# Output projection of an attention layer: four blocks at the end of a strip, or one after every second head pair of the next strip

## The reference

```python
x = x + attn(layernorm(x))     # 16 heads of 64, causal, width 1024, 2048 tokens
x = x + ffn(layernorm(x))      # activations quantised to 8 bits, weights to {-1, 0, 1}

# attn
q, k, v = x @ Q_w + Q_b, x @ K_w + K_b, x @ V_w + V_b      # per head
logits = q k^T / sqrt(64);  causal mask;  scores = softmax(logits)
attn = scores @ v
return einsum('bqhd,hdm->bqm', attn, O_w) + O_b            # the output projection
```

## Time and profile before

| | us |
|---|---|
| median of 2 runs | 4601.35 (4590.81 to 4611.88) |
| profiled execution | 4576.53 |
| its span, slowest core (core 5) | 4575.0 |
| the other cores | 4530.7 to 4571.6 |
| mean granted TensorE clock, by core | 0.748 to 0.753 of full speed |
| TensorE matmuls busy | 2803.8 (61% of the span) |
| VectorE busy | 1714.8 (37%) |
| ScalarE busy | 1032.6 (23%) |

### The profile page before, as it was taken

The page is one execution under the profiler, slowest core; times in us unless marked ns, Lnnn a source line. Parts: engine busy times, 40 slices in busy tenths (PEclk is TensorE's granted clock), DMA queues, the critical chain, the costliest instruction groups (busy, mean ns, idle before and its releaser), DMA issues. The chain is left out here.

```text
span 4575.0 us, 49341 instructions; the slowest of 8 cores (4530.7 to 4575.0 us)
## 1 busy us (share of the span) xinstructions
PE 2803.8 (61%) x17576; PEld 1453.1 (32%) x17576; DVE 1714.8 (37%) x3961; ACT 1032.6 (23%) x1127; POOL 45.5 (1%) x68
## 2 busy tenths in 40 slices
PE   0078557778712126767776377567778447778675
PEld 0023123334311114444442133133334234445342
DVE  1121243332233455645555122232111446564643
ACT  0001024447421131001010011024647231111010
POOL 0000000000000000000000000000000000000000
PEclk9988656665655559889898788665665678989889
DMA  7610022111164203445454410000000023545444
GB/s 125 175 33 19 19 92 83 66 61 42 48 173 141 107 19 78 121 120 147 120 148 136 154 32 14 19 28 6 15 19 1 10 42 83 148 123 150 128 129 156
DMA packets 472110, 380.91 MB, mean 83 GB/s; under 512 B 340674, under 2 KB 373570, under 8 KB 466756
## 3 DMA queue, kind: packets, MB, share of 16 engines
q1 hardware_dynamic: 460612, 335.81, 25.8%
q0 software_dynamic: 11264, 41.95, 2.9%
HBM read 335.77 MB, written 41.94 MB: 83 GB/s over the span
## 5 line engine op out<-in xcount | busy, mean ns | idle before, releaser
L80 ACT ACTIVATE b_pt<-b_lp,b_cb 128x1024 bf16<-128x1024 f32 (+3 forms) x640 | 622.1, 986 | 556.7 <-PE b_lp L80 355.2
L80 PE MATMUL c_op<-c_w2b,c_hq 128*128 128x512 bf16 x2048 | 516.9, 398 | 250.4 <-DMA c_w2b<-w2t_s 187.5
L80 PE MATMUL c_hp<-c_xq,c_w1b 128*128 128x257 bf16 x4096 | 521.4, 282 | 66.9 <-ACT c_H L80 58.3
L80 PE MATMUL b_av<-V,b_pt 128*128 128x65 bf16 x5120 | 376.9, 237 | 208.1 <-ACT b_pt L80 146.9
L80 PEld LDWEIGHTS c_hp<-c_xq,c_w1b 128*128 128x128 bf16 x4096 | 408.9, 101 | 203.1 <-issue 103.7
L80 ACT ACTIVATE c_H<-c_hp,c_cb 128x512 bf16<-128x512 f32 x256 | 175.9, 687 | 1249.4 <-DVE c_H L80 598.2
L80 PEld LDWEIGHTS b_av<-V,b_pt 128*128 128x128 bf16 x5120 | 296.1, 124 | 421.4 <-issue 421.3
L80 PE MATMUL b_lp<-Q,K 64*128 64x512 bf16 x1280 | 369.2, 589 | 11.0 <-DVE x L80 9.3
L80 PEld LDWEIGHTS c_op<-c_w2b,c_hq 128*128 128x128 bf16 x2048 | 197.6, 101 | 547.3 <-issue 354.0
L80 DVE TENSOR_TENSOR c_H<-c_hp,c_g1b 128x514 bf16<-128x514 f32 x256 | 176.8, 691 | 466.6 <-PE c_hp L80 465.9
L80 DVE MEMSET b_pt<- 128x256 bf16 (+2 forms) x192 | 93.1, 485 | 621.7 <-PE b_lp L80 551.5
(11 more groups left out here) (124 smaller groups left out, 2443.2 us busy)
## 6 DMA issues: line engine op xcount, KB each, us to landing
c_w2b<-w2t_s SPq DMA_DIRECT2D x256, 512.0 KB, 5.3
c_w1b<-w1t_s SPq DMA_DIRECT2D x128, 512.0 KB, 4.3
pw_stg<-w SPq DMA_DIRECT2D x32, 1024.0 KB, 4.9
wq_st<-w SPq DMA_DIRECT2D x16, 2048.0 KB, 9.1
a_xt<-x SPq DMA_DIRECT2D x32, 512.0 KB, 3.5
b_xr<-x SPq DMA_DIRECT2D x32, 512.0 KB, 3.6
out<-c_obf POOLq DMA_DIRECT2D x32, 512.0 KB, 3.3
wq_s<-p_wbf POOLq DMA_DIRECT2D x16, 512.0 KB, 8.0
```

What stands on the lines that cost most here:

```text
L80: h = getattr(eng, en["name"])(*en["args"], **en["kwargs"])
```

## The change

The attention buffer `atok` keeps its size in bytes but becomes two halves of bf16, one for each parity of the strip, so that a strip can be normalised into one half while the other is projected. The four blocks at the end of a strip go into a function, `emit_oproj(pp, v, rg)`. In strips 1 to 3, after pairs 0, 2, 4 and 6, one block of the strip before is emitted; after the last strip its own four follow. A block uses one region of `AVps2` (`rg`, always 0) for both the transposes and the output, no longer `Lps`; a list `reg_free` holds for each region the VectorE count from which it is free. The transposes are bf16 matmuls against the bf16 identity. The condition on `ve_x2` in `emit_logits` (line 612) stays in the text; it now refers to the last block of the strip before, or to none in strip 1. The wait of a new region's first AV matmuls, on `reg_free`, takes the place of those on `ve_pn2` and `ve_aT2`.

```diff
@@ -529,7 +529,7 @@
         qsq = es_b.enter_context(nc.sbuf_tensor(f"b_sq{s}", [128, 512], BF16))
         smf = es_b.enter_context(nc.sbuf_tensor(f"b_sm{s}", [128, 16], F32))
         ptil = es_b.enter_context(nc.sbuf_tensor(f"b_pt{s}", [128, 2048], BF16))
-        atok = es_b.enter_context(nc.sbuf_tensor(f"b_at{s}", [128, 4 * 1024], F32))
+        atok = es_b.enter_context(nc.sbuf_tensor(f"b_at{s}", [128, 2 * 4096], BF16))
         attT = es_b.enter_context(nc.sbuf_tensor(f"b_tt{s}", [128, 1024], BF16))
         zrec = es_b.enter_context(nc.sbuf_tensor(f"b_zr{s}", [128, 8], F32))
         xre = es_b.enter_context(nc.sbuf_tensor(f"b_xr{s}", [128, 2 * D], F32))
@@ -592,8 +592,7 @@
                 nc.psum_tensor(f"b_av{s}", [128, 2048], F32))
             sc_exp = [0, 0]
             ve_pn = 0
-            ve_pn2 = [0, 0]
-            ve_aT2 = 0
+            reg_free = [0, 0]
             ve_x2 = 0
             tn_tT = 0
             dl_x = [0] * NT
@@ -601,6 +600,51 @@
                 dl_x[u] = dlb[u % 2].inc(r.sync.dma_start(
                     out=xre[:, (u % 2) * D:(u % 2 + 1) * D],
                     in_=t_x[s, u * 128:(u + 1) * 128, :]), 16)
+            def emit_oproj(pp, v, rg):
+                nonlocal ve_x2, tn_tT
+                u = 4 * pp + v
+                ah2 = (pp % 2) * 4096
+                rb = rg * 1024
+                r.wait(r.tensor, ve, ve_pn)
+                r.wait(r.tensor, ve, reg_free[rg])
+                for c in range(8):
+                    tn.inc(r.tensor.matmul(
+                        AVps2[:, rb + c * 128:rb + (c + 1) * 128],
+                        atok[:, ah2 + v * 1024 + c * 128:
+                             ah2 + v * 1024 + (c + 1) * 128],
+                        ident_bf[:, :], start=True, stop=True,
+                        skip_group_check=True))
+                tn_tT = tn.v
+                r.wait(r.vector, tn, tn_tT)
+                ve_aT = ve.inc(r.vector.tensor_copy(
+                    attT[:, :], AVps2[:, rb:rb + 1024]))
+                r.wait(r.tensor, ve, ve_aT)
+                for half in range(2):
+                    hs = half * 512
+                    for c in range(8):
+                        tn.inc(r.tensor.matmul(
+                            AVps2[:, rb + hs:rb + hs + 512],
+                            attT[:, c * 128:(c + 1) * 128],
+                            OWb[:, c * 1024 + hs:c * 1024 + hs + 512],
+                            start=(c == 0), stop=False))
+                    tn.inc(r.tensor.matmul(
+                        AVps2[:, rb + hs:rb + hs + 512], ones1b[0:1, :],
+                        ob_row[0:1, hs:hs + 512], start=False, stop=True))
+                tn_o = tn.v
+                r.wait(r.vector, tn, tn_o)
+                r.wait(r.vector, dlb[u % 2], dl_x[u])
+                ve_x2 = ve.inc(r.vector.tensor_add(
+                    x2[:, u * D:(u + 1) * D],
+                    xre[:, (u % 2) * D:(u % 2 + 1) * D],
+                    AVps2[:, rb:rb + 1024]))
+                reg_free[rg] = ve_x2
+                nu = u + 2
+                if nu < NT:
+                    r.wait(r.sync, ve, ve_x2)
+                    dl_x[nu] = dlb[nu % 2].inc(r.sync.dma_start(
+                        out=xre[:, (nu % 2) * D:(nu % 2 + 1) * D],
+                        in_=t_x[s, nu * 128:(nu + 1) * 128, :]), 16)
+
             if s == 0:
                 stats_load(0)
                 stats_load(1)
@@ -668,9 +712,7 @@
                                 AF.Exp, scale=0.125, bias=Cbias[:, hp:hp + 1]))
                         r.wait(r.tensor, sc, sc_exp[lb])
                         if kc == 0:
-                            r.wait(r.tensor, ve, ve_pn2[hp % 2])
-                            if hp < 2 and p > 0:
-                                r.wait(r.tensor, ve, ve_aT2)
+                            r.wait(r.tensor, ve, reg_free[hp % 2])
                         ab = (hp % 2) * 1024
                         for hh in range(2):
                             for qs in range(4):
@@ -693,57 +735,22 @@
                         bass.AP(AVps2[:, :].tensor, ab + 64,
                                 [[2048, 128], [512, 2], [65, 4], [1, 1]])))
                     ve.inc(r.vector.drain())
+                    ah = (p % 2) * 4096
                     for hh in range(2):
                         for qs in range(4):
                             ve_pn = ve.inc(r.vector.tensor_single_scalar(
-                                atok[:, qs * 1024 + (2 * hp + hh) * 64:
-                                     qs * 1024 + (2 * hp + hh + 1) * 64],
+                                atok[:, ah + qs * 1024 + (2 * hp + hh) * 64:
+                                     ah + qs * 1024 + (2 * hp + hh + 1) * 64],
                                 AVps2[:, ab + hh * 512 + qs * 65:
                                       ab + hh * 512 + qs * 65 + 64],
                                 zrec[:, hh * 4 + qs:hh * 4 + qs + 1], ALU.mult))
-                    ve_pn2[hp % 2] = ve_pn
+                    reg_free[hp % 2] = ve_pn
                     if s == 0:
                         stats_step(p * 8 + hp)
-                for v in range(4):
-                    u = 4 * p + v
-                    r.wait(r.tensor, ve, ve_pn)
-                    r.wait(r.tensor, sc, sc.v)
-                    if v == 0:
-                        r.wait(r.tensor, ve, ve_x2)
-                    for c in range(8):
-                        tn.inc(r.tensor.transpose(
-                            AVps2[:, c * 128:(c + 1) * 128],
-                            atok[:, v * 1024 + c * 128:v * 1024 + (c + 1) * 128],
-                            ident_f32[:, :]))
-                    tn_tT = tn.v
-                    r.wait(r.vector, tn, tn_tT)
-                    ve_aT = ve.inc(r.vector.tensor_copy(attT[:, :],
-                                                        AVps2[:, 0:1024]))
-                    ve_aT2 = ve_aT
-                    r.wait(r.tensor, ve, ve_aT)
-                    for half in range(2):
-                        hs = half * 512
-                        for c in range(8):
-                            tn.inc(r.tensor.matmul(
-                                Lps[:, hs:hs + 512],
-                                attT[:, c * 128:(c + 1) * 128],
-                                OWb[:, c * 1024 + hs:c * 1024 + hs + 512],
-                                start=(c == 0), stop=False))
-                        tn.inc(r.tensor.matmul(
-                            Lps[:, hs:hs + 512], ones1b[0:1, :],
-                            ob_row[0:1, hs:hs + 512], start=False, stop=True))
-                    tn_o = tn.v
-                    r.wait(r.vector, tn, tn_o)
-                    r.wait(r.vector, dlb[u % 2], dl_x[u])
-                    ve_x2 = ve.inc(r.vector.tensor_add(
-                        x2[:, u * D:(u + 1) * D],
-                        xre[:, (u % 2) * D:(u % 2 + 1) * D], Lps[:, 0:1024]))
-                    nu = u + 2
-                    if nu < NT:
-                        r.wait(r.sync, ve, ve_x2)
-                        dl_x[nu] = dlb[nu % 2].inc(r.sync.dma_start(
-                            out=xre[:, (nu % 2) * D:(nu % 2 + 1) * D],
-                            in_=t_x[s, nu * 128:(nu + 1) * 128, :]), 16)
+                    if p >= 1 and hp % 2 == 0:
+                        emit_oproj(p - 1, hp // 2, 0)
+            for v in range(4):
+                emit_oproj(NP - 1, v, 0)
             if s == 0:
                 for n in range(NP * 8, 32):
                     stats_step(n)
```

## The result

The changed kernel is slower by 0.66%: the ratio to the kernel before is 1.0066, 95% interval 1.0045 to 1.0086, with medians of 4620.2 and 4588.3 us over 33 and 32 runs. (In some executions, whatever the kernel, the cores of one die run at a lower granted clock and take longer; the ratios leave such executions out, the medians don't, and of the last experiment's profile cores 0 to 3 alone are read, for this reason.) The forecast was 1.6%, or 74 us; measured are some 30. The direction was right, and the forecast more than twice the measured size.

What follows compares the result with a forecast made beforehand. ScalarE and TensorE wait in turn with nothing queued ahead for ScalarE, so blocks between pairs cost their whole time. Terms -210.3 + 285.4 - 5.4 + 4.4 = +74 us, scaled to 4676 us; range 4630 to 4712 us.

Steps and rivals of the forecast that it cites:

- What bounds the stage: Attention stage: nothing is queued ahead for ScalarE at a pair's end, so work put there adds its whole time.
- The 24 blocks: After pairs 0, 2, 4, 6 of strips 1 to 3: each copies a burst's first block, together +285.4 us.
- bf16 in the normalisation at no cost: Normalisation writing bf16, eight instructions of 1.63 us in all: taken as 0, bounds 0 and -19 us.
- After a block: Pair behind a block: no wait for the add, clock still high, 0.3 us gained at 18 more places, -5.4 us.
- The last burst: End of each sequence: one region makes transposes wait for the add, 0.9 us more a later block; +4.4 us in all.
- rival C: Strips 1 to 3: blocks keep the clock high through attention, -40 us, 4561 us, 0.9% faster; chance 10%.
- Rival B: Single blocks: clock stays low through every block, 13 to 13.9 us each, +117 us, 4719 us, 2.6% slower; chance 15%.
- Rival D: Blocks between pairs: hidden behind busy ScalarE, nearly all 210 us gone, 4390 us, 4.6% faster; chance 3%.

Runs made afterwards that it cites:

- the last experiment: `spread_halves` plus useless matmuls in pairs of strips 1 to 3, four ahead of the first AV matmuls and two on the diagonal: ratio 0.943, median 4318.0 us.
- spread_halves: Changed kernel with each block dealt out inside two pairs, between key blocks, and the last burst alternating regions: ratio 0.9548, median 4367.0 us, stage time 1035.8 us.
- experiment 2: Kernel before, with block output in the AV tile's second region, so the next logits don't wait for the add: ratio 0.996, stage time 1223.0 us.
- experiment 3: Experiment 2's kernel with six or twelve useless matmuls behind each burst between strips: stage time 1224.2 or 1235.2 us, against 1223.0 without.
- experiment 1: Changed kernel, with the logits behind each block waiting for the block's add again: ratio 1.025 to the kernel before, stage time 1333.4 us.
- experiment 4: Changed kernel with eight useless matmuls behind each of the 24 blocks: stage time 1325.3 us, +57.4 us.
- experiment 5: Experiment 2's kernel with useless matmuls in pairs of strips 1 to 3, at start and diagonal, then start only: stage times 1108.8 and 1110.9 us, against 1223.0.

## Why the prediction was right and wrong, point by point

- **What bounds the stage: right.** Nothing is queued for ScalarE at a pair's end, so a block there is paid whole. `spread_halves` shows it from the other side: with the same work behind queued logits the stages take 201 us less than with the bursts, part of it by the higher clock.
- **The 24 blocks: right.** +285.4 forecast, +279.3 measured; single ones 10.4 to 12.8 us over the cores. The first block of a burst was a good copy of them, to the reduction that hides the faster transposes in sequence 0. The eight bf16 matmuls took 1.01 us, as the bf16 transposes of the earlier trace rows at the low clock, and being plain matmuls did not bring the rise nearer: it came 4.5 us after a block's first output matmul in the mean, 4.4 us before the change. (The prediction says that no row has a transpose in transpose mode; those of the earlier trace rows are `transpose` calls of the program, and whether they use that mode the trace doesn't show.)
- **bf16 in the normalisation at no cost: right.** 276 ns an instruction in the mean, before and after.
- **"After a block": wrong, and this is the miss.** I priced the high clock behind a block by the six pairs behind bursts, 0.3 us each. It is about 2 us, 47 us in all instead of 5. The two other errors, 6 us too much for the blocks and 5 too little for the last bursts, cancel by luck. The step took a burst to be a stronger form of a block ("after 28 us of dense matmuls it lasted under ten microseconds of attention"). Experiments 2 and 3 show that it isn't: what ends the high clock is mostly the idle time at a pair's start (experiments 1, 4 and 5), and whether that does it depends on where the start lies to the rise. All bursts ended at about the same distance from their rise (22 to 24 us), so six equal rows were nearer to one observation than to six.
- **The skill's rule.** The Trainium skill ("TensorE: Matmul & The Clock Gate", "Loop structure matters more than you think") says that a long DMA wait between matmuls costs the clock, a copy on VectorE between dense stretches none. By it I had rival C, at 10%. The trace of after agrees in part: clock 0.69 over 700 to 1210 us, where the kernel before has 0.61 there. C was half true: its mechanism acted in the typical case, up to the pair's end and not beyond; that it did not turn the direction of the result is partly luck, for it hung on where the pairs' starts lay. Its price for a pair at full clock, 8%, was also low: 15.1 against 17.5 us (experiment 5) is 14%.
- **The last burst:** +4.4 forecast, +9.4 measured. The wait for the region was sized rightly (0.95 us); what was left out is that the longer gap lets the clock fall inside the burst.
- **Rival B (low clock through every block): wrong.** The rise came inside 186 of 192 blocks, 1.8 to 2.1 us before the last matmul in the mean of a strip. **Rival D:** not what this order does; it is what `spread_halves` does.
- **Range:** 4630 to 4712 us; measured 4620. Its lower end should have reached to C's 4561, whose mechanism was written down and got 10%; I had cut it off as one of the cases left out. The windows of the changed kernel and of the kernel before (core 3, core 5) over the same stretch, clock 0.69 and 0.61:

```profile
700.00:1210.00 510.00, 360.20 (x3242) 177.28 (x3238) 147.98 (x310) 274.59 (x278) 0.00 (x0) 0.69 0.17 57
...
700.00:1210.00 510.00, 399.86 (x3341) 199.60 (x3339) 154.05 (x331) 286.01 (x288) 0.00 (x0) 0.61 0.17 58
```

## What to carry to other kernels

Work moved between two dependent stages is hidden only if something for the waiting engine is queued ahead of it; look at what stands on either side in the same queue before you count it as overlapped. Where TensorE runs between its two clock levels, price a change from pairs at either level (here 12.5 / 17.5 / 22.6 against 10.4 / 14.7 / 18.9 us) and keep both ends in the range, for small shifts in time flip between them. And look for the one short idle place that recurs: filling it may be worth more than removing work.

## What the runs showed of the hardware that I had not expected

- Matmuls without any use, four in each pair of strips 1 to 3, 48 pairs on a core, took 112 us off the stage time (1223.0 to 1110.9), and the granted clock was at its high level nearly throughout (0.91 to 0.98 in windows of core 5 in these strips, instead of 0.53 to 0.65).
- The idle time that decides is short: 1.06 us at the low level, 1.25 us at the high one (experiment 1's row), ahead of a pair's first AV matmuls. With it alone the clock sometimes stayed and sometimes fell; with 1.5 us more in front it fell in all 46 pairs that started 3.75 us or more after the rise, without it in 2 of 54 (experiments 1 and 4).
- Whether it stays can hang on a small shift in the place of the pair's start: 1.3 us more behind a burst, and 42 of 48 bursts left the high clock up for 6 us or longer, where 3 of 48 had (experiment 3); in the changed kernel the two kinds part within a fraction of a microsecond. What rule the chip follows in between, these runs don't settle.
